# One block for the feed-forward network and the second attention, with their border woven together

## The chip, the cores and the metric

The kernel runs on one core of a Trainium2 chip. The metric is device time in microseconds (us), the median of several runs of the whole program; 1610.68 us before the change.

## The reference, cut to what matters

Two sequences of 512 tokens, width 512, all in float32, pass through four pre-normalised layers:

```python
x = x + _L0_attn_ref(_layernorm(x, axis=-1), L0_attn_wq, L0_attn_wk, L0_attn_wv, L0_attn_wo)
x = x + _L0_ffn_ref(_layernorm(x, axis=-1), L0_ffn_gate_t, L0_ffn_up_t, L0_ffn_down_t, L0_ffn_gate_s, L0_ffn_up_s, L0_ffn_down_s)
x = x + _L1_attn_ref(_layernorm(x, axis=-1), L1_attn_w_qkv, L1_attn_b_qkv, L1_attn_w_out, L1_attn_b_out)
x = x + _L1_ffn_ref(_layernorm(x, axis=-1), L1_ffn_A, L1_ffn_B, L1_ffn_Wr)
```

The change touches the border of the second line and the third. The network is `silu(x @ gate) * (x @ up)`, 1792 wide, times `down`. The second attention has 32 heads of 16, an ALiBi slope, a causal mask and biases on its projections.

## The kernel before, in words

Each layer is a phase in a `Block` of its own. A block ends with a barrier of all five engines; only then does the next phase's first instruction stand, on any engine or queue. Every float32 product is three matmuls: an operand is held as a rounded part `hi` and a rest `lo`, and `product` issues hi*hi, hi*lo and lo*hi (L64 to L66). Who makes `hi` and `lo` differs: ScalarE and VectorE for activations, GpSimd for the second attention's weights.

**The network** (`ffn0_phase`). 14 chunks of 128 of the 1792 hidden columns are made one after the other for both sequences. The first sequence's four output tiles are summed in four PSUM banks as the chunks come. The second sequence's hidden columns (`hidden1`) are kept, and its four output tiles are made after the last chunk, each in one run of 14 products = 42 matmuls, into the same four banks. So the first of them waits until VectorE has read the first bank (`out_scaled`). VectorE scales each finished tile by `down_s` (L953), adds it to `x` (L955) and takes its mean and variance (L76, L78).

**The norm** (`LayerNorm`). When all eight token tiles have their moments: a square root on ScalarE (L135), a reciprocal (L111), then for each tile a subtract-and-multiply on VectorE (L117), four transposes on TensorE (L150), `xT_hi` on ScalarE (L138) and `xT_lo` on VectorE (L124). TensorE waits for all eight tiles before its next matmul.

**The second attention** (`attention1_phase`). Heads are taken in 4 chunks of 8; a chunk has 16 units, 8 heads for each sequence, and `step(c, s)` runs a software pipeline: it scores unit s+3 (L1323), turns the probabilities of unit s+1 (L1336), attends unit s (L1348), and carries one piece of side work, such as the projection of the queries, keys or values of one sequence (`SIDE1`). Queries and keys are not used as they are made: SyncE writes them to DRAM (`write_out`), and GpSimd's queue reads them back into `stacked_q` and `stacked_k` in another layout, together with the slopes (`read_back`, L1234 to L1240). The first unit of each chunk and sequence waits for both. Steps 7 to 15 of chunk -1 are the preamble. GpSimd runs in program order: the first weights' halves, a memset of `stacked_q` (L1275), the read-backs of steps 7 and 8, that of step 15, eight additions of the output bias to `x` (L1283), the next query weights, and only then the read-back of step 0's keys.

## Time and profile before

| | before |
|---|---|
| median of 3 runs | 1610.68 us (1609.86 to 1612.18) |
| profiled execution's own time | 1609.08 us |
| its span, first to last instruction | 1607.2 us |
| TensorE (PE) busy | 1469.5 us, 91% |
| VectorE (DVE) busy | 1013.9 us, 63% |
| ScalarE (ACT) busy | 857.9 us, 53% |
| GpSimd (POOL) busy | 534.8 us, 33% |

"Busy" counts the instructions that compute. The shares are means over four phases: the first attention ends near 838 us, the network near 1089, the second attention near 1475. All times below are us from the start of the span of this one execution.

### The profile page before, as it was taken

Reading aid. Unit: us, or ns where it says so; the run is one execution under the profiler, and the core shown is the slowest. Engines: PE = TensorE matmul, PEld = TensorE weight load, DVE = VectorE, ACT = ScalarE, POOL = GpSimd, SP = SyncE. Lnnn points to the kernel's source line nnn. Section 1 sums busy time; section 2 is a strip of 40 time slices with the busy share of each in tenths; the row PEclk is TensorE's granted clock in tenths of the full one; section 3 lists DMA queues with packets and bytes.
Section 4 is the critical chain, followed back from the end, with each engine's and each line's share of the span. In section 5 each row is a group of like instructions: output and inputs, shape, how many; then the busy total and the mean of one; then the engine's idle time right before and its main releaser. Section 6 shows DMA issues by size and latency. Waiting matters only on the chain. (4 is left out here: it accounts for less than half of the span.)

```text
span 1607.2 us, 25387 instructions
## 1 busy us (share of the span) xinstructions
PE 1469.5 (91%) x7696; PEld 1208.1 (75%) x7696; DVE 1013.9 (63%) x2543; ACT 857.9 (53%) x2181; POOL 534.8 (33%) x465
## 2 busy tenths in 40 slices
PE   5999999999999999999778999995879999986798
PEld 3778888888888888888666888873667777764587
DVE  6676767676666676666544333344768888897543
ACT  2666555665566565556514233202768888894210
POOL 3673555545456554462400000005331313110500
PEclk9999999999999999999998999997889999997899
DMA  4010010101001010000002111005333444422000
GB/s 147 20 47 14 27 40 20 39 13 33 26 26 33 13 33 26 26 7 8 20 6 100 59 59 59 0 0 129 74 73 83 86 78 90 74 42 98 17 21 27
DMA packets 37468, 71.97 MB, mean 45 GB/s; under 512 B 4976, under 2 KB 5360, under 8 KB 36848
## 3 DMA queue, kind: packets, MB, share of 16 engines
q1 hardware_dynamic: 29664, 55.35, 11.3%
q0 software_dynamic: 7728, 15.73, 6.0%
q8 instruction: 33, 0.54, 0.1%
q14 instruction: 43, 0.35, 0.1%
HBM read 60.58 MB, written 10.49 MB: 44 GB/s over the span
## 5 line engine op out<-in xcount | busy, mean ns | idle before, releaser
L728 ACT ACTIVATE a_probs<-a_probs,a_least 128x512 f32<-128x512 f32 (+3 forms) x256 | 142.9, 559 | 175.6 <-DVE a_least L629 168.3
L377 POOL TENSOR_TENSOR a_rotated<-a_by_cos,a_by_sin 128x512 f32<-128x512 f32 x80 | 103.4, 1292 | 248.3 <-DVE a_by_sin L652 246.2
L637 DVE TENSOR_TENSOR a_probsT_lo<-a_ps_turn,a_probsT_hi 128x512 fp32r<-128x512 f32 (+3 forms) x256 | 118.7, 485 | 71.2 <-ACT a_probsT_hi L736 69.7
L736 ACT CAST a_probsT_hi<-a_ps_turn 128x512 fp32r<-128x512 f32 (+3 forms) x256 | 101.3, 426 | 102.0 <-PE a_ps_turn L526 102.0
L1532 ACT ACTIVATE a_probs<-a_probs,a_least 128x128 f32<-128x128 f32 (+3 forms) x256 | 142.3, 561 | 12.5 <-DVE a_least L1435 9.7
L1435 DVE CUSTOM_DVE_ANT_0 a_probs<-a_ps_score,a_causal 128x128 f32<-128x128 f32 (+3 forms) x256 | 117.2, 486 | 40.8 <-PE a_ps_score L1323 31.0
L782 ACT ACTIVATE a_probs<-a_probs,a_inverse 128x128 f32<-128x128 f32 (+3 forms) x256 | 123.2, 553 | 8.7 <-DVE a_inverse L690 7.5
L64 PE MATMUL a_ps_out<-a_wo_hi,a_attended_hi 128*128 128x512 f32 x256 | 105.5, 412 | 17.8 <-POOL a_wo_lo L371 15.6
L629 DVE CUSTOM_DVE_ANT_0 a_probs<-a_ps_score,a_causal 128x512 f32<-128x512 f32 (+2 forms) x192 | 101.1, 551 | 28.8 <-PE a_ps_score L66 28.7
L387 POOL TENSOR_TENSOR a_query_lo<-a_rotated,a_query_hi 128x512 fp32r<-128x512 f32 x64 | 82.6, 1290 | 105.8 <-ACT a_query_hi L748 105.8
L1443 DVE TENSOR_TENSOR a_probsT_lo<-a_ps_turn,a_probsT_hi 128x384 fp32r<-128x384 f32 (+1 forms) x192 | 108.9, 595 | 2.7 <-ACT a_probsT_hi L1541 2.6
L671 DVE TENSOR_TENSOR x<-a_ps_out,x 128x512 f32<-128x512 f32 x64 | 44.3, 692 | 104.9 <-PE a_ps_out L66 104.9
L64 PE MATMUL a_ps_proj<-xT_hi,a_wq_hi 128*128 128x512 f32 x256 | 110.3, 431 | 0.0
L1541 ACT CAST a_probsT_hi<-a_ps_turn 128x384 fp32r<-128x384 f32 (+1 forms) x192 | 85.7, 510 | 37.5 <-PE a_ps_turn L1336 37.4
L1336 PE MATMUL a_ps_turn<-ident,a_probs 128*128 128x128 f32 x640 | 93.2, 277 | 12.3 <-ACT a_probs L1532 12.2
L526 PE MATMUL a_ps_turn<-ident,a_probs 128*128 128x128 f32 x640 | 101.7, 273 | 1.1 <-ACT a_probs L782 1.1
L65 PE MATMUL a_ps_out<-a_wo_lo,a_attended_hi 128*128 128x512 f32 x256 | 102.7, 401 | 0.0
L66 PE MATMUL a_ps_out<-a_wo_hi,a_attended_lo 128*128 128x512 f32 x256 | 102.3, 400 | 0.0
L66 PE MATMUL a_ps_proj<-xT_hi,a_wq_lo 128*128 128x512 f32 x256 | 101.6, 397 | 0.0
L65 PE MATMUL a_ps_proj<-xT_lo,a_wq_hi 128*128 128x512 f32 x256 | 101.2, 395 | 0.0
L1323 PE MATMUL a_ps_score<-a_stacked_k,a_stacked_q 128*128 128x128 f32 (+3 forms) x256 | 77.6, 380 | 24.2 <-DMA a_stacked_k<-in_slope 13.2
L1216 POOL MEMSET a_zeros<- 128x512 f32 x1 | 0.5, 524 | 289.0 <-POOLq L811 289.0
(250 smaller groups left out, 4205.6 us busy)
## 6 DMA issues: line engine op xcount, KB each, us to landing
a_raw<-in_wq SPq DMA_DIRECT2D x36, 256.0 KB, 2.6
a_raw<-in_wo SPq DMA_DIRECT2D x36, 256.0 KB, 2.7
a_stacked_q<-a_spill_q POOLq DMA_DIRECT2D x48, 128.0 KB, 5.0
a_stacked_k<-a_spill_k POOLq DMA_DIRECT2D x24, 256.0 KB, 4.6
f_raw<-in_gate SPq DMA_DIRECT2D x14, 256.0 KB, 2.8
f_raw<-in_up SPq DMA_DIRECT2D x14, 256.0 KB, 3.0
f_raw<-in_down SPq DMA_DIRECT2D x14, 256.0 KB, 3.5
a_raw<-in_wk SPq DMA_DIRECT2D x12, 256.0 KB, 2.7
```

What stands on the lines that cost most here:

```text
L64: nc.tensor.matmul(out, left[0], right[0], start=start, stop=False)
L65: nc.tensor.matmul(out, left[0], right[1], start=False, stop=False)
L66: return nc.tensor.matmul(out, left[1], right[0], start=False, stop=stop)
L377: nc.gpsimd.tensor_tensor(rotated[:], by_cos[:], by_sin[:], ALU.add).then_inc(rotation_added, 1)
L526: last = nc.tensor.transpose(ps_turn[:, t % 2, (i - t) * P:(i - t + 1) * P], probs[:, u % 2, at:at + P], m.ident[:])
L637: nc.vector.tensor_tensor(probsT[1][:, t % 2, 0:w], ps_turn[:, t % 2, 0:w], probsT[0][:, t % 2, 0:w].bitcast(F32), ALU.subtract).then_inc( ...
L728: nc.scalar.activation(tile, tile, ACT.Exp, bias=least[:, slot, i:i + 1], scale=-1.0, accum_out=total[:, slot, i:i + 1]).then_inc(exp_done, 1)
L736: nc.scalar.copy(probsT[0][:, t % 2, 0:w], ps_turn[:, t % 2, 0:w]).then_inc(turned_hi, 1)
L782: nc.scalar.activation(tile, tile, ACT.Copy, scale=inverse[:, slot, i:i + 1]).then_inc(probs_ready, 1)
L1435: nc.vector.tensor_tensor_reduce(out=probs[:, u % 4, at:at + w], in0=ps_score[:, i % 2, 0:w], in1=causal[:, SEQ - w:SEQ], scale=-float(HD1 ...
L1443: nc.vector.tensor_tensor(probsT[1][:, u % 2, at], ps_turn[:, t, 0:TURNED_WIDTH[t]], probsT[0][:, u % 2, at].bitcast(F32), ALU.subtract).t ...
L1532: nc.scalar.activation(tile, tile, ACT.Exp, bias=least[:, u % 4, i:i + 1], scale=-1.0, accum_out=total[:, u // 4 % 2, i, u % 4:u % 4 + 1]) ...
```

## The change

The two phases become one function, `ffn0_attention1_phase`, with one block; the network becomes a class `Ffn0`. Both share one SBUF area and the same eight PSUM banks. `stacked_q`, `stacked_k`, `values`, `probs` and others lie in the place of the network's `down` and `hidden1` chunks, so a part is free once the last output tile has used a chunk (`chunk_free`); weights and small buffers lie in the place of `gate`, `up` and `raw`. The second sequence's tiles go to the banks of `ps_gate` and `ps_up` (`out_bank`). The norm of the second attention is cut in two halves of four tiles, one for each sequence, with a PSUM bank for each tile. The instructions keep their sizes and numbers, except that the load of `pick` and the memset of `stacked_q` are cut in two.

```diff
+    def second_sequence(self, pe, t, chunks):
+        nc, down, hidden1 = self.nc, self.down, self.hidden1
+        at = slice((t - QT) * P, (t - QT + 1) * P)
+        for f in chunks:
+            mm = product(nc, self.out_bank(t), (hidden1[0][:, f, at], hidden1[1][:, f, at]),
+                         (down[0][:, f, :], down[1][:, f, :]), f == 0, f == FC - 1)
+            if f == FC - 1:
+                mm.then_inc(self.out_done, 1)
+            elif t == NT - 1:
+                mm.then_inc(self.chunk_free, 1)
...
@@ tensor
-            norm.tensor(pe)
-            pe.wait_ge(pick_in, 16)
+            half = FC // 2
+            ffn.tensor(pe)
+            ffn.second_sequence(pe, 4, range(FC))
+            ffn.second_sequence(pe, 5, range(half))
+            norm.turn(pe, 0)
+            ffn.second_sequence(pe, 5, range(half, FC))
+            norm.ready(pe, 0)
+            side_work(-1, 7)
+            ffn.second_sequence(pe, 6, range(half))
+            side_work(-1, 8)
+            ffn.second_sequence(pe, 6, range(half, FC))
+            ffn.second_sequence(pe, 7, range(FC))
+            side_work(-1, 9)
...
+            pe.wait_ge(pick_in[0], 16)
+            pe.wait_ge(ffn.out_scaled, 6)
+            step(-1, 13)
+            side_work(-1, 10)
+            norm.turn(pe, 1)
+            pe.wait_ge(pick_in[1], 16)
             each_chunk(pe, step)
...
@@ vector
-            norm.vector(dve)
-            dve.wait_ge(consts_in, 16 * 3)
+            ffn.vector(dve)
+            for t in range(QT):
+                ffn.add_out(dve, t)
+            norm.shift(dve, 0)
+            norm.invert(dve, 0)
+            for t in range(QT):
+                norm.normalise(dve, t)
+            for t in range(QT):
+                norm.split(dve, t)
+            norm.normal_free(dve, 0)
+            ffn.add_out(dve, 4)
+            ffn.add_out(dve, 5)
+            dve.wait_ge(bias_in, 16)
...
+            step(-1, 8)
+            step(-1, 9)
+            ffn.add_out(dve, 6)
+            ffn.add_out(dve, 7)
+            norm.shift(dve, 1)
+            dve.wait_ge(causal_in, 16)
+            step(-1, 13)
+            norm.invert(dve, 1)
+            for t in range(QT, NT):
+                norm.normalise(dve, t)
+            step(-1, 11)
+            for t in range(QT, NT):
+                norm.split(dve, t)
+            norm.normal_free(dve, 1)
             each_chunk(dve, step)
...
@@ sync
+            ffn.sync(sp)
+            sp.dma_start(bias[:], dram["bias1"]).then_inc(bias_in, 16)
+
+            sp.wait_ge(ffn.weights_split, 3 * FC)
             for w, name in enumerate(("wq1", "wk1", "wv1")):
                 sp.dma_start(raw[:, w, :], dram[name][0]).then_inc(raw_in[w], 16)
...
@@ gpsimd
+            pool.wait_ge(ffn.made, 2 * FC)
             for what in ("wq", "wk", "wv"):
                 split(1, piece_count(0, what), what)
...
+            def prepare(b):
+
+                pool.wait_ge(ffn.chunk_free, 2 * b + 2)
+                pool.dma_start(stacked_q[96:P, b].rearrange("p a e n -> p (a e n)"),
+                               dram["pick"][:, b * 2 * PAIRS * SEQ:(b + 1) * 2 * PAIRS * SEQ]).then_inc(pick_in[b], 16)
+                nc.gpsimd.memset(stacked_q[0:96, b].rearrange("p a e n -> p (a e n)").bitcast(F32), 0.0).then_inc(stack_zero, 1)
+                pool.wait_ge(stack_zero, b + 1)
...
-            for s in (7, 8, 15):
-                read_back(-1, s)
+            prepare(0)
+            read_back(pool, -1, 7)
+            pool.wait_ge(ffn.chunk_free, 5)
+            read_back(pool, -1, 8)
+            prepare(1)
+            read_back(pool, -1, 15)
```

`second_sequence` appends tiles 4 to 7, the second sequence's, as matmuls; `side_work(-1, 7)`, `(-1, 8)`, `(-1, 9)` are the first projections of queries, keys and values; `step(-1, 13)` is the scoring of unit 0, and `side_work(-1, 10)` turns the values.

What moves on GpSimd, the engine that reads queries and keys back. Its first read-backs, before the change: the memset of both sequences' `stacked_q`, six DMAs of queries, then three of keys and one of slopes, which wait for the written keys.

```order
L1275 MEMSET a_stacked_q 96x8192
L1234 DMA a_stacked_q<-a_spill_q 16x4x512 [waits a1_stack_zero,a1_query_out]
L1234 DMA a_stacked_q<-a_spill_q 16x4x512 x5
L1238 DMA a_stacked_k<-a_spill_k 32x4x512 [waits a1_keys_out]
L1238 DMA a_stacked_k<-a_spill_k 32x4x512 x2
L1240 DMA a_stacked_k<-in_slope 32x2048
```

The same place after the change:

```order
L1333 DMA a_stacked_q<-in_pick 32x4096 [waits f0_chunk_free]
L1335 MEMSET a_stacked_q 96x4096
L1219 DMA a_stacked_q<-a_spill_q 16x4x512 [waits a1_stack_zero,a1_query_out]
L1219 DMA a_stacked_q<-a_spill_q 16x4x512 x5
L1223 DMA a_stacked_k<-a_spill_k 32x4x512 [waits f0_chunk_free,a1_keys_out]
L1223 DMA a_stacked_k<-a_spill_k 32x4x512 x2
L1225 DMA a_stacked_k<-in_slope 32x2048
```

The load of `pick`, which stood at the phase's start, has come behind the chunk count and ahead of a memset of half the size. Further down in GpSimd's program, at the second sequence's read-backs, before the change:

```order
L1234 DMA a_stacked_q<-a_spill_q 16x4x512 [waits a1_query_out]
L1234 DMA a_stacked_q<-a_spill_q 16x4x512 x5
L1283 TENSOR_TENSOR x<-x,a_out_bias 128x512 [waits ln_normal_done,a1_consts_in]
L1283 TENSOR_TENSOR x<-x,a_out_bias 128x512 x7
L1251 TENSOR_TENSOR a_wq_hi<-a_raw,a_zeros 128x512 [waits a1_wq_in,a1_side_made]
L1253 TENSOR_TENSOR a_wq_lo<-a_raw,a_wq_hi 128x512 [waits a1_piece_hi]
L1238 DMA a_stacked_k<-a_spill_k 32x4x512 [waits a1_keys_out]
L1238 DMA a_stacked_k<-a_spill_k 32x4x512 x2
L1240 DMA a_stacked_k<-in_slope 32x2048
```

After the change:

```order
L1219 DMA a_stacked_q<-a_spill_q 16x4x512 [waits a1_stack_zero,a1_query_out]
L1219 DMA a_stacked_q<-a_spill_q 16x4x512 x5
L1223 DMA a_stacked_k<-a_spill_k 32x4x512 [waits a1_keys_out]
L1223 DMA a_stacked_k<-a_spill_k 32x4x512 x2
L1225 DMA a_stacked_k<-in_slope 32x2048
L1305 TENSOR_TENSOR x<-x,a_out_bias 128x512 [waits ln_normal_done,a1_out_bias_in]
L1305 TENSOR_TENSOR x<-x,a_out_bias 128x512 x7
L1296 TENSOR_TENSOR a_wq_hi<-a_raw,a_zeros 128x512 [waits a1_wq_in,a1_side_made]
L1298 TENSOR_TENSOR a_wq_lo<-a_raw,a_wq_hi 128x512 [waits a1_piece_hi]
```

The key read-back now stands ahead of the eight bias additions and the two weight halves. On ScalarE, from the square root's table to the first exponentials of the second attention, after the change (`f_ps_out` and `f_ps_up` are the shared banks):

```order
L155 ACT_TABLE_LOAD
L155 ACTIVATE ln_deviation<-ln_shifted 128x4 [waits ln_var_done]
L162 CAST xT_hi<-f_ps_out 128x4x128 [waits ln_turned_done] x4
L1666 CAST a_query_hi<-a_biased_q 128x512 [waits a1_side_read]
L1666 CAST a_keys_hi<-a_biased_k 128x512 [waits a1_side_read]
L155 ACTIVATE ln_deviation<-ln_shifted 128x4 [waits ln_var_done]
L1679 COPY a_values_turned<-f_ps_out 128x512 [waits a1_side_made]
L1683 CAST a_values<-f_ps_out 128x32x16 [waits a1_side_made]
L162 CAST xT_hi<-f_ps_up 128x4x128 [waits ln_turned_done] x2
L162 CAST xT_hi<-f_ps_out 128x4x128 [waits ln_turned_done] x2
L1641 ACT_TABLE_LOAD
L1641 ACTIVATE a_probs,a_total<-a_probs,a_least 128x128 [waits a1_score_masked]
```

Before, the eight casts of `xT_hi` all stood ahead of the queries, and the exponentials' table load stood right behind the cast of `a_values`; now four casts stand between them.

## Rows read from the trace of the kernel before

**Rows 1.** Busy time of each engine by stretch; PEclk is the granted clock
```profile
core 0: us, PE busy (x) PEld busy (x) DVE busy (x) ACT busy (x) POOL busy (x), PEclk, DMA share, GB/s
...
1048.00:1087.00 39.00, 38.62 (x168) 31.47 (x168) 15.01 (x28) 0.00 (x0) 0.00 (x0) 1.00 0.00 0
1087.00:1103.00 16.00, 8.64 (x34) 5.89 (x33) 13.80 (x22) 6.18 (x10) 8.00 (x8) 0.63 0.63 165
...
1177.00:1475.00 298.00, 268.28 (x1680) 209.12 (x1678) 254.47 (x746) 248.93 (x710) 53.77 (x78) 0.98 0.35 67
```

**Rows 2.** Timeline of TensorE over the border: start, duration, instruction, idle before
```profile
1048.38 0.47 PE L64 MATMUL f_ps_out<-f_down_hi,f_hidden_hi 128*128 128x512 f32 x1 [0.99 <-DVE f_hidden L953]
1048.69 0.40 PE L65 MATMUL f_ps_out<-f_down_lo,f_hidden_hi 128*128 128x512 f32 x1
...
1086.69 0.40 PE L66 MATMUL f_ps_out<-f_down_hi,f_hidden_lo 128*128 128x512 f32 x1
1092.14 1.97 PE L150 MATMUL a_ps_turn<-ident,a_probs 128*128 128x128 f32 x8 [5.06 <-DVE a_probs L117]
...
1103.56 0.63 PE L65 MATMUL a_ps_side<-xT_lo,a_wq_hi 128*128 128x512 f32 x1
1103.98 0.63 PE L66 MATMUL a_ps_side<-xT_hi,a_wq_lo 128*128 128x512 f32 x1
...
1127.97 0.77 PE L1323 MATMUL a_ps_score<-a_stacked_k,a_stacked_q 128*128 128x128 f32 x2 [10.25 <-DMA a_stacked_k<-in_slope]
...
1133.02 1.70 PE L1336 MATMUL a_ps_turn<-ident,a_probs 128*128 128x128 f32 x7
```

**Rows 3.** Timeline of TensorE around the second sequence's first unit
```profile
1159.08 0.98 PE L1336 MATMUL a_ps_turn<-ident,a_probs 128*128 128x128 f32 x7 [1.46 <-ACT a_probs L1532]
...
1163.23 0.98 PE L1336 MATMUL a_ps_turn<-ident,a_probs 128*128 128x128 f32 x7 [0.52 <-ACT a_probs L1532]
1172.35 0.77 PE L1323 MATMUL a_ps_score<-a_stacked_k,a_stacked_q 128*128 128x128 f32 x2 [8.14 <-issue]
...
1176.53 0.93 PE L1336 MATMUL a_ps_turn<-ident,a_probs 128*128 128x128 f32 x7
```

**Rows 4.** Timeline of GpSimd: its memset, its read-backs, the bias additions
```profile
1103.99 6.93 POOL L1275 MEMSET a_stacked_q<- 96x8192 f32 x1
1114.14 3.07 POOL L1234 DMA_DIRECT2D a_stacked_q<-a_spill_q  x6 [3.22 <-DMA a_spill_q<-a_query_lo]
1120.83 1.62 POOL L1238 DMA_DIRECT2D a_stacked_k<-a_spill_k  x3 [3.61 <-DMA a_spill_k<-a_keys_lo]
1122.43 0.52 POOL L1240 DMA_DIRECT2D a_stacked_k<-in_slope  x1
1152.58 9.98 POOL L1283 TENSOR_TENSOR x<-x,a_out_bias 128x512 f32<-128x512 f32 x8
...
1166.69 0.51 POOL L1240 DMA_DIRECT2D a_stacked_k<-in_slope  x1
```

**Rows 5.** VectorE beside GpSimd: an operation with both inputs in SBUF
```profile
301.94 1.29 POOL L377 TENSOR_TENSOR a_rotated<-a_by_cos,a_by_sin 128x512 f32<-128x512 f32 x1
...
302.15 1.23 DVE L629 CUSTOM_DVE_ANT_0 a_probs<-a_first_tile,a_causal 128x128 f32<-128x128 f32 x1 [0.19 <-DVE a_first_tile L625]
```

**Rows 6.** Landing of all DMAs into `a_stacked_k`
```profile
DMA to landing us min/median/max: 3.3/5.1/7.6
```

**Rows 7.** Single operations of VectorE and ScalarE that the sum uses
```profile
1099.86 0.53 DVE L117 TENSOR_SCALAR a_probs<-x,moments,ln_inverse 128x512 f32<-128x512 f32 x1
...
1131.03 0.08 DVE L1435 DVE_READ_ACCUMULATOR2_ANT a_least<- 128x1 f32 x1
...
1101.60 0.58 ACT L138 CAST xT_hi<-a_ps_score 128x512 fp32r<-128x512 f32 x1 [0.47 <-PE a_ps_score L150]
...
1118.37 1.28 ACT L1532 ACT_TABLE_LOAD   x1
```

**Rows 8.** The page's group of all exponentials of the second attention
```profile
L1532 ACT ACTIVATE a_probs<-a_probs,a_least 128x128 f32<-128x128 f32 (+3 forms) x256 | 142.3, 561 | 12.5 <-DVE a_least L1435 9.7
```

623 lines of the change are left out of this document (338 added, 285 removed).

## The prediction, on record before the changed kernel ran

> **What bounds the kernel now.** I began with the page, where TensorE is busy for 91% of the span, so that a border between two phases matters only where TensorE stands still or runs at the lower clock. The chain that ended last lies in the last phase alone and says nothing of this border. So I took the busy time by stretch, then TensorE's timeline, then those of the engines that release it.
>
> Until 1087 TensorE issues the second sequence's 168 matmuls without a gap, at a granted clock of 1.00 (2.4 GHz) [rows 1]. They start 0.23 us apart: 166 steps in 38.0 us [rows 2]. Nothing else is behind them: GpSimd does nothing in that stretch and ScalarE nothing [rows 1]. Then come, one after the other, the last tile's moments, the barrier, the norm, three projections, and the trip of queries and keys through DRAM. TensorE idles 5.06 us, does the norm at a clock of 0.63 on average [rows 1, 2], projects at a pitch of 0.42 us (1103.56 to 1103.98, 1.2 GHz), and idles 10.25 us more until the slopes, the last of the keys' DMAs, have landed [rows 2]. From the last of the 168 matmuls (1086.69) to the first score (1127.97) are 41.3 us, in which TensorE has only 36 matmuls and 36 transposes to do.
>
> A second gap follows. At 1164.2 TensorE wants the second sequence's first score and gets it at 1172.35, 8.14 us later [rows 3]. The row names no releaser, but GpSimd's rows do: the keys' read-back stands behind 9.98 us of bias additions and two weight halves, its slopes are issued at 1166.69 and the score comes 5.66 us after that [rows 3, 4]. After 1177 TensorE, VectorE and ScalarE are busy for 90, 85 and 84% [rows 1], and no gap of this size is left.
>
> **The change part by part.** The instructions are the same, so the sum is of waits. I walk along the new path in the times of this trace.
>
> *Start of tile 4.* It no longer waits 0.99 us for `out_scaled` [rows 2], only for `hidden_lo`, which VectorE ends directly before the scaling of the first bank, so some 0.7 us of the gap could go. But the first weights' halves now run on GpSimd at that moment, and `hidden_lo` has both inputs in SBUF. Such an operation of VectorE took 1.23 us beside a running GpSimd operation, for 128x128, and ended with it [rows 5]. So I give back most of the 0.7: start at 1048.2, bounds 1047.7 and 1048.9. The Trainium skill has this as a rule (SBUF — State Buffer, "Who interferes with whom"): a VectorE instruction with two SBUF inputs contends with a GpSimd instruction that reads SBUF, and one in a two-port mode with any GpSimd instruction. It speaks against this change, which puts GpSimd's splits and memsets beside VectorE's additions to `x` and its norm; rows 5 agree with it, and by it each addition beside a split may wait for the end of that split.
>
> The additions have room for that. VectorE does the first four tiles in about 9 us (28 instructions, seven tiles' worth, are busy for 15.0 us [rows 1]) and the norm's half in 3 more, so normalised tiles are there by 1060, or by 1062 if GpSimd costs it 2 us; TensorE asks for them after 63 matmuls, at 1048.2 + 14.4 = 1062.6. The norm of the first half therefore costs TensorE only its 16 transposes at 0.14 us (7 take 0.98) [rows 3], 2.2 us, and casts and `xT_lo` lie under the 21 matmuls (4.8 us) behind them. The queries' and keys' additions, halves and writes lie under tile 6, with some 10 us to spare before they are read back.
>
> *Start of tile 7.* 126 matmuls of tiles 4 to 6 and 24 of queries and keys, 150 x 0.229 = 34.35 us, and 2.2: 1084.75. Two chunks of tile 7 more (6 matmuls, 1.4 us) release GpSimd at 1086.15.
>
> *The read-back, the path from here on.* The load of `pick` 0.5 us as any issue (0.52); half of the memset's 6.93 us, 3.47; six query issues 3.07; three key issues 1.62 [rows 4]: the slopes are issued at 1094.8. From that issue to the first score were 5.54 us before (1122.43 to 1127.97) [rows 2, 4] and 5.66 at the other gap: first score at 1100.4. Before, it was at 1127.97: 27.6 us are won here. Meanwhile TensorE ends tile 7 and the values at 1084.75 + 54 x 0.229 = 1097.1 and waits some 3.3 us; that is what is left of 41 us. Bounds: the landings into `a_stacked_k` were 3.3 to 7.6 us [rows 6]; here 1.75 MB of queries and keys are issued back to back, so the upper end is open: -2.2 to +2.1 us.
>
> The Trainium skill prices it otherwise (DMA: Bandwidth & Descriptors, "Anatomy of one DMA — SWDGE (gpsimd) path"): 2.0 us, plus the bytes at 436 bytes per ns, for a DMA of GpSimd. For the slopes' 0.26 MB that is 2.6 us, an estimate by that page, and TensorE's own work would then end last, at 1097.1: the whole gain would be 3.3 us larger. The rows, 5.5 us twice, decide for the sum.
>
> *From the first score to the first turn.* Before, 5.05 us (1127.97 to 1133.02) [rows 2]. Now the second half of the norm stands between, and with it what was parallel becomes serial: the four masks of unit 0 take 3.1 us (1131.03 against 1127.97) [rows 2, 7]; reciprocal and first normalised tile 0.8 (0.53 for the tile); then four tiles, by TensorE at the low clock 4.3 us (8 transposes 1.97, the rows' pitch of 1.06 a tile), by VectorE's 0.53 a tile 2.1; the last cast 0.58; then ScalarE's table load of 1.28, which lay hidden in a wait before; then four exponentials of 0.56 [rows 2, 7, 8]. With the mean of the two paces, 3.2: 3.1 + 0.8 + 3.2 + 0.6 + 1.3 + 2.25 = 11.25, and 0.2 for hand-overs. The first turn is at 1111.9, against 1133.02: **21.1 us** remain of the 27.6. Bounds: pace of the transposes ±1.1, the landing -2.2 and +2.1, VectorE and GpSimd ±0.5: 18 to 24.
>
> *The second gap.* The stretch from 1133.02 to 1163.23 has the same rows in both kernels. Where the score waits now, GpSimd issues the keys' read-back directly behind the queries' (which ends at 1152.58): the keys' three DMAs and the slopes are issued by 1155 (3.07 and 1.62 us of issues as before, if the written keys have landed by then, as an estimate), landed at 1160.7 by the 5.66, before the 1164 at which they are wanted. Then the next turn follows after the pace of the step before, 1163.23 - 1159.08 = 4.15, at 1167.4 instead of 1176.53 [rows 3]: 9.1 us, in which the return from the low clock is contained. The keys' 1 MB now share the queues with the next weights and the queries, so I take off 0.6: **8.5 us**, bounds 5 (three more us of landing eat the margin and some) and 9.4. The bias additions and weight halves, now behind, end some 13 us later, near 1168; the next chunk's queries want them at 1175 in the same shifted times. That margin hides them; if it were gone, it would cost what it falls short.
>
> Sum: 21.1 + 8.5 = 29.6 us. Against the profiled execution's own time, 1609.08, that is 1579.5. The median of the runs stands 1.6 above it, so **1581.1 us**.
>
> **The rivals.** A measurement of this kernel tells some 0.2%, 3.2 us, from no change.
>
> (a) *Both gaps close as summed*: 1577 to 1586. Chance 0.63.
>
> (b) *The second gap stays in part, 8.5 becomes 2 to 5.* The keys wait behind the queries' and weights' transfers, or GpSimd, in program order, is late with something that is queued behind it. For it: the 1164 of demand is only 3.5 us after my landing, and the longest landing was 7.6 [rows 6]. Then 2 to 5 us of the 8.5 are won, 1584.6 to 1587.6, and with a late first landing up to 1590. Chance 0.17.
>
> (c) *Landings are as quick as the page has them, or the clock stays up*: TensorE idles under 1 us before the first score and does the transposes at 2.4 GHz: 3.3 + 1.1 more, 1573 to 1577. Against it: two gaps that took 5.5 us. Chance 0.10.
>
> (d) *The gain is mostly given back by VectorE.* It now carries the adds of tiles 6 and 7, the norm's halves and the masks in one fixed order, and each waits for the one before; a step in the wrong order (shift of half 1 stuck behind GpSimd's memset of 3.47 us, then ScalarE's root, then its copy of the values) lies just under the landing of 1100.4. Were it 5 to 15 us late: 1586 to 1596. Chance 0.07.
>
> (e) *Slower.* The stretch now issues projections, transposes and tiles of three kinds. If TensorE's clock fell to 1.2 GHz in it, each of the 204 matmuls would take 0.42 instead of 0.229 us, up to +39 us, 1620; from 155 matmuls at the low clock on (29.6 / 0.19) the kernel is slower. Against it: the clock stayed at 1.00 over the 0.99 us gap at 1047 [rows 1, 2], and the new order has no longer one before 1097. Chance 0.03.
>
> **How the numbers follow.** The likeliest case gives 1581.1, its own range 1577 to 1586. With (c)'s nearer half and most of (b) the range is 1575 to 1589; outside are (d), (e) and the far ends. Faster by over 0.2% covers (a), (b), (c) and nearly all of (d): 0.96; within 0.2%: 0.01; slower 0.03.
>
> **What would show it.** In the trace of the changed kernel: 168 + 36 matmuls with no gap over 1 us from 1048 to 1097; a gap of 2 to 5 us before the first score, released by the slopes' DMA; the first turn of probabilities near 1112, behind a table load of ScalarE; no gap of 8 us at the ninth unit's score, near 1142; and from there the same rows some 30 us earlier. I am wrong if the first score comes before 1097 or after 1103, if VectorE releases TensorE inside the woven stretch for more than 1 us, or if a gap reappears at a later chunk's first score, where GpSimd's program is the same as before.

## The result: 1591.2 us, 19.6 us faster, where 29.6 were forecast

The changed kernel took 1591.22 us in the median of its first four runs (1589.31 to 1595.56), beside 1610.85 before: a ratio of 0.988, interval 0.986 to 0.990. The sign and the place of the gain were as forecast; the gain was a third smaller than forecast, and 1591.2 lies outside the range of 1575 to 1589. In a second set of runs the same kernel took 1588.2 us beside 1610.0 (0.987, 0.985 to 0.988), 21.8 us faster and just inside that range. The profiled execution is the slowest of the first four: 1595.56 us by its own time, a span of 1593.4 us. It already runs 2.7 us late when the border begins (its last halves of the network's hidden values are 2.7 us behind those of before), so 2.7 us are taken off where its times are held against those of before.

TensorE's timeline over the border and the two gaps (start, duration, instruction, idle before it and what ended that) answers to [rows 2, 3]:

```profile
1050.75 0.50 PE L64 MATMUL f_ps_gate<-f_chunks 128*128 128x512 f32 x1 [0.68 <-DVE f_chunks L973]
...
1106.51 0.76 PE L1387 MATMUL f_ps_gate<-a_stacked_k,a_stacked_q 128*128 128x128 f32 x2 [7.46 <-DMA a_stacked_k<-in_slope]
...
1118.41 1.73 PE L1400 MATMUL f_ps_out<-ident,a_probs 128*128 128x128 f32 x7 [1.92 <-ACT a_probs L1641]
...
1144.52 0.98 PE L1400 MATMUL f_ps_out<-ident,a_probs 128*128 128x128 f32 x7 [1.45 <-ACT a_probs L1641]
...
1148.66 0.98 PE L1400 MATMUL f_ps_out<-ident,a_probs 128*128 128x128 f32 x7 [0.55 <-ACT a_probs L1641]
1150.66 0.47 PE L1387 MATMUL f_ps_gate<-a_stacked_k,a_stacked_q 128*128 128x128 f32 x2 [1.01 <-issue]
...
1155.89 1.14 PE L1387 MATMUL f_ps_gate<-a_stacked_k,a_stacked_q 128*128 128x384 f32 x2 [3.85 <-DVE a_least L1529]
...
1157.90 1.44 PE L1400 MATMUL f_ps_out<-ident,a_probs 128*128 128x128 f32 x7
```

Between 1050.75 and 1106 no row of TensorE shows an idle time: the woven stretch holds. The first score still waits for the slopes, as forecast, but 7.46 us and not 3.3. The ninth unit's score (1150.66) no longer waits 8 us but 1.01; its third and fourth parts wait 3.85 us more, and not for a DMA but for VectorE's mask.

GpSimd's timeline, against [rows 4]:

```profile
1088.49 0.65 POOL L1333 DMA_DIRECT2D a_stacked_q<-in_pick  x1 [32.00 <-PE f_ps_up L66]
1089.13 3.54 POOL L1335 MEMSET a_stacked_q<- 96x4096 f32 x1
1093.33 3.02 POOL L1219 DMA_DIRECT2D a_stacked_q<-a_spill_q  x6 [0.66 <-POOL a_stacked_q L1335]
...
1097.95 0.52 POOL L1225 DMA_DIRECT2D a_stacked_k<-in_slope  x1
1098.45 0.52 POOL L1333 DMA_DIRECT2D a_stacked_q<-in_pick  x1
...
1135.06 3.01 POOL L1219 DMA_DIRECT2D a_stacked_q<-a_spill_q  x6 [32.57 <-DMA a_spill_q<-a_query_lo]
1142.10 1.61 POOL L1223 DMA_DIRECT2D a_stacked_k<-a_spill_k  x3 [4.03 <-DMA a_spill_k<-a_keys_lo]
1143.70 0.51 POOL L1225 DMA_DIRECT2D a_stacked_k<-in_slope  x1
1144.23 9.90 POOL L1305 TENSOR_TENSOR x<-x,a_out_bias 128x512 f32<-128x512 f32 x8
1154.09 1.25 POOL L1296 TENSOR_TENSOR a_wq_hi<-a_raw,a_zeros 128x512 fp32r<-128x512 f32 x1
```

The bias additions, a stretch without a pause from 1144.23 to 1154.09, now stand exactly over the time in which VectorE divides the first half of the attention. VectorE's timeline there:

```profile
1149.43 0.63 DVE L1546 TENSOR_REDUCE a_summed<-f_ps_up 128x256 f32<-128x512 f32 x1
1150.16 5.47 DVE L1551 TENSOR_TENSOR a_result<-a_summed,a_inverse 128x256 f32<-128x256 f32 x1
1155.55 0.28 DVE L1529 CUSTOM_DVE_ANT_0 a_probs<-f_ps_gate,a_causal 128x128 f32<-128x128 f32 x1
```

The multiply at L1551 has both inputs in SBUF. Its group over the whole trace, of the kernel before and then of the changed one (minimum, median and maximum in ns, first and last start):

```profile
L1457 DVE TENSOR_TENSOR a_result<-a_summed,a_inverse x16: 424/425/1492, 1164.7 to 1461.3; 128x256 f32<-128x256 f32 x16
```

and changed:

```profile
L1551 DVE TENSOR_TENSOR a_result<-a_summed,a_inverse x16: 424/426/5466, 1150.2 to 1448.6; 128x256 f32<-128x256 f32 x16
```

Thirteen of the sixteen take 0.43 us at most, two take 0.99 and 1.44 beside GpSimd's weight halves, and the one beside the bias additions takes 5.47. It ends at 1155.63, 0.29 us behind the first weight half (`wq_hi`, 1154.09 to 1155.34), and behind that half GpSimd pauses for the first time since 1144.23, for 0.08 us. In VectorE's order the masks of the ninth unit stand behind it, and TensorE, which needs a free score bank, behind those.

Where the 13.8 us of difference between the two spans come from: to the first turn of probabilities 14.61 (1133.02 to 1118.41), at the second gap 4.06 (from the turn before it to the turn behind it 13.30 before [rows 3], 9.24 now), in the expert phase, whose code is the same, 1.59, and of that 6.42 are lost again between 1157.90 and the end of the second attention (305.1 us against 298.7), and 0.04 between the gaps.

### The profile page after: what moved, and what is told of

Its sections match the earlier page's. It is cut to its first block and busy times, and to the rows that moved or that the text cites. A ratio compares the mean times of both kernels' runs of the same rounds, so it can differ in the third digit from the quotient of the medians.

```text
span 1593.4 us, 25389 instructions
## 1 busy us (share of the span) xinstructions
PE 1469.0 (92%) x7696; PEld 1212.6 (76%) x7696; DVE 1021.9 (64%) x2545; ACT 857.5 (54%) x2182; POOL 536.5 (34%) x467
## 3 DMA queue, kind: packets, MB, share of 16 engines
HBM read 60.58 MB, written 10.49 MB: 45 GB/s over the span
## 5 line engine op out<-in xcount | busy, mean ns | idle before, releaser
L1529 DVE CUSTOM_DVE_ANT_0 a_probs<-f_ps_gate,a_causal 128x128 f32<-128x128 f32 (+3 forms) x256 | 117.1, 486 | 32.8 <-PE f_ps_gate L1387 22.9
L1537 DVE TENSOR_TENSOR a_probsT_lo<-f_ps_out,a_probsT_hi 128x384 fp32r<-128x384 f32 (+1 forms) x192 | 108.9, 596 | 2.3 <-ACT a_probsT_hi L1650 2.2
L1400 PE MATMUL f_ps_out<-ident,a_probs 128*128 128x128 f32 x640 | 94.4, 280 | 13.8 <-ACT a_probs L1641 13.7
L1650 ACT CAST a_probsT_hi<-f_ps_out 128x384 fp32r<-128x384 f32 (+1 forms) x192 | 85.7, 510 | 32.7 <-PE f_ps_out L1400 32.7
L555 PE MATMUL a_ps_turn<-ident,a_probs 128*128 128x128 f32 x640 | 101.5, 273 | 1.1 <-ACT a_probs L811 1.1
L1387 PE MATMUL f_ps_gate<-a_stacked_k,a_stacked_q 128*128 128x128 f32 (+3 forms) x256 | 77.8, 382 | 20.7 <-DMA a_stacked_k<-in_slope 12.3
L1400 PEld LDWEIGHTS f_ps_out<-ident,a_probs 128*128 128x128 f32 x640 | 75.2, 143 | 25.2 <-ACT a_probs L1641 11.3
```

The costliest lines, as they stand in the source:

```text
L555: last = nc.tensor.transpose(ps_turn[:, t % 2, (i - t) * P:(i - t + 1) * P], probs[:, u % 2, at:at + P], m.ident[:])
L1400: last = nc.tensor.transpose(ps_turn[:, t, to:to + P], probs[:, u % 4, at:at + P], m.ident[:])
L1529: nc.vector.tensor_tensor_reduce(out=probs[:, u % 4, at:at + w], in0=ps_score[:, i % 2, 0:w], in1=causal[:, SEQ - w:SEQ], scale=-float(HD1 ...
L1537: nc.vector.tensor_tensor(probsT[1][:, u % 2, at], ps_turn[:, t, 0:TURNED_WIDTH[t]], probsT[0][:, u % 2, at].bitcast(F32), ALU.subtract).t ...
```

## The experiments

Fifteen variants and the changed kernel once more. Times are medians. "The landing" is the time from the issue of the slopes' DMA to the first score of TensorE, unless said otherwise; "the step over the gap" is the time from the turn of probabilities before the second gap to the turn behind it; "the release" is the issue of the first load of `pick` or, where GpSimd's memset comes first, the start of that memset.

### The changed kernel again

> The changed kernel, nothing altered. Its profiled execution was its slowest run (1595.56 us against 1589.31 to 1592.02 in the others), and lost 4.0 us at the scores of the third chunk and 2.0 at those of the fifth, where TensorE waited 2.76 and 2.12 us for the slopes and then ran at 1.2 GHz for a while; before the change the same waits were 1.43 and 1.49 and the clock stayed up. Theory that this is chance in the landings (they differ from run to run): median 1590 to 1592 and, in this profile, at least one of the two waits under 1.6 us with no slow clock behind it. Rival, that the change itself makes these landings late: both waits above 2 us again. The first score (1106.5, 8.5 us after the slopes' issue) and the multiply of a_result of 5.47 us at 1150 come back in either case.

1588.22 us (1585.18 to 1589.06), ratio 0.9869 (0.9854 to 0.9883). The first score comes 8.0 us behind the slopes' issue, the multiply takes 5.88 us and the step over the second gap 9.65. The waits that the expectations place in "the third chunk" and "the fifth", or in "the chunks 2 and 4", are those of the second sequence's first score in the second and in the third of the four chunks (at 1237.84 and 1322.90 in the profile of the result). Here they are 2.57 and 1.52 us, with the granted clock at 1.00 behind both. The second is under 1.6, as the theory of chance asks, but the median lies 1.8 us below its range, and both waits are again above those of the profile before (1.43 and 1.49). So this run does not settle it. What stands before the border differs from trace to trace too: the last casts of the network's hidden values begin between 1043.0 and 1049.0 us in the sixteen traces of changed kernels, whose code is the same up to there, and at the fortieth instruction of ScalarE (63.1 to 67.3 us) 4.2 us of that are already there.

### The second part of the change alone

In the kernel before, only the order of GpSimd in the first chunk:

```diff
                 more = not isinstance(c, int) or c < CHUNKS1 - 1
+                first = isinstance(c, int) and c == 0
+                if first:
+                    read_back(c, 0)
+                    pool.wait_ge(consts_in, 16 * 3)
+                    pool.wait_ge(m.ln_semaphores[LN_SEMAPHORES.index("normal_done")], 3 * NT)
+                    for t in range(NT):
+                        nc.gpsimd.tensor_tensor(m.x[:, t, :], m.x[:, t, :], out_bias[:], ALU.add).then_inc(bias_added, 1)
                 if more:
                     wait(pool, side_made, side_count(c - 1, 15))
                     split(c + 2, piece_count(c + 1, "wq"), "wq")
-                read_back(c, 0)
+                if not first:
+                    read_back(c, 0)
...
-            pool.wait_ge(consts_in, 16 * 3)
-            pool.wait_ge(m.ln_semaphores[LN_SEMAPHORES.index("normal_done")], 3 * NT)
-            for t in range(NT):
-                nc.gpsimd.tensor_tensor(m.x[:, t, :], m.x[:, t, :], out_bias[:], ALU.add).then_inc(bias_added, 1)
             chunk(0)
```

> The kernel before with one thing of the change: in the first chunk GpSimd reads the keys back ahead of the bias additions and of the split of the first weights. Theory A, VectorE's multiply into a_result with two inputs in SBUF is held by the bias additions of GpSimd that now run beside it, so the second gap shrinks by 4 us and not by 8.5: 1606 to 1608, with that multiply at 4 to 6 us. Theory B, my prediction: the gap closes, 8.5 us won, 1601.5 to 1603, with the multiply at 0.4 to 1.5 us.

1607.01 us over 12 runs (1602.0 to 1610.2), ratio 0.9979 (0.9968 to 0.999): 3.0 us won. That fits theory A. The step over the gap is 8.69 us (13.30 before), and VectorE's multiply is the slow one:

```profile
1166.29 4.92 DVE L1461 TENSOR_TENSOR a_result<-a_summed,a_inverse 128x256 f32<-128x256 f32 x1
```

### The first part alone

```diff
                 if first:
-                    read_back(pool, c, 0)
                     add_out_bias()
                 if more:
                     wait(pool, side_made, side_count(c - 1, 15))
                     split(c + 2, piece_count(c + 1, "wq"), "wq")
-                if not first:
-                    read_back(pool, c, 0)
+                read_back(pool, c, 0)
```

> The changed kernel with GpSimd's old order in the first chunk: bias additions and the split of the first weights ahead of the keys' read-back; all else as changed. That is the first part of the change alone. By the trace of the changed kernel the second part is worth 4.0 us: 1594 to 1596. By my prediction it is worth 8.5: 1599 to 1600.

1592.32 us (1588.7 to 1595.3), ratio 0.9899 (0.9885 to 0.9913). That is 17.7 us under the kernel before, and 4.1 above the changed kernel in the same set of runs. The wait of the ninth score is back, 7.87 us, the multiply takes 0.97 us at most, and the step over the gap is 13.05. So the two parts are worth 17.7 and 4.1 us, not 21.1 and 8.5. It came out 1.7 us below what was expected for 4.0.

### The bias additions where GpSimd is idle

```diff
             prepare(1)
+            add_out_bias()
             read_back(pool, -1, 15)
...
                 if first:
                     read_back(pool, c, 0)
-                    add_out_bias()
```

> The changed kernel with the bias additions directly behind the preparation of the second half of the queries' buffer, in the 30 us in which GpSimd waits for the next queries; no other line altered. Theory A (the additions hold VectorE's multiply, and the masks and TensorE's score behind it): the multiply falls from 5.47 to about 0.4 to 1.5 us, the wait of 3.85 us at TensorE and the slow clock behind it go, 4 to 5 us won, 1585.5 to 1587.5. Theory B (the multiply is slow for another reason, or something else then holds the score): no change, 1590 to 1592. It is slower if the additions now hold VectorE's norm or casts instead: over 1592.

1585.04 us (1584.6 to 1587.4), 3.2 under the changed kernel. The additions run from 1108.5 to 1118.4. Nothing else was touched, and the multiply is short:

```profile
1148.37 0.93 DVE L1551 TENSOR_TENSOR a_result<-a_summed,a_inverse 128x256 f32<-128x256 f32 x1
```

The turns of TensorE on both sides of the gap are at 1146.87 and 1151.99: a step of 5.12 us, where 9.24 and 9.65 were, and 4.8 forecast. The granted clock stays at 1.00 behind the score; in the changed kernel it was 0.50 from 1156 to 1158. This shows the cause of the missing 4 us: the multiply beside the additions. The keys' landing still holds the score 1.45 us here, within that step. The additions start when the second half's normalised tiles are done, and VectorE's `xT_lo`, which now run beside them, lose nothing by it: 0.69 us each, as in the changed kernel.

### The second load of `pick` out of the way

```diff
+            pool.wait_ge(score_made, 12)
             prepare(1)
...
-            pe.wait_ge(pick_in[1], 16)
...
+                    if isinstance(cu, int) and (cu, u) == (0, HPC):
+                        pe.wait_ge(pick_in[1], 16)
```

> The changed kernel with GpSimd's preparation of the second half of the queries' buffer (its load of pick, 0.5 MB, and its memset) held until three units are scored; TensorE waits for that load only at the ninth unit. In the changed kernel this load is issued 0.5 us behind the slopes and shares the queues with them. Theory P, it delays the slopes: they land 5.5 to 6.5 us after their issue instead of 8.5, and the first score comes 2 to 3 us earlier against the end of tile 7, for 1585.5 to 1587. Theory Q, it is the 1.75 MB of queries, keys and slopes issued back to back: still 8 to 9 us, and the time is that of the changed kernel, 1588 to 1591. In either case VectorE's shift of the second half, 3.75 us before, takes under 0.5 us, and gives nothing, since it is done long before its inverse is wanted.

1590.67 us (1589.2 to 1592.3): nothing won. The landing is 7.71 us, against 8.56, 8.00, 8.23 and 8.28 in the four traces until then, but 7.76 and 7.89 in two that ran in one set with it and leave the load in place. Theory P's 5.5 to 6.5 us are refuted; the landing is a little below the 8 to 9 of theory Q. What this load costs the slopes is within what the landings differ by from trace to trace. VectorE's shift of the second half takes 0.17 us here, as expected.

### The exponential's table early

```diff
             step(-1, 11)
+            nc.scalar.activation(total[:, 1, 3, 3:4], norm.shifted[:, norm.columns(1)][:, 0:1], ACT.Exp)
             norm.round(act, 1)
```

> The changed kernel with one more instruction of ScalarE: an exponential of one element a partition, behind the copy of the first values, whose result nobody reads. It pulls the load of the exponential's table into the time in which ScalarE waits for the second half's transposes. If that load (1.28 us) and what follows it set the first turn, as the prediction's serial sum has it, the first turn comes 1.0 to 1.3 us sooner behind the first score (11.9 us before): 10.6 to 10.9, and the median falls by about as much, 1587 to 1590. If VectorE or TensorE sets that turn: no change.

The median, 1589.54 us (1585.6 to 1590.5), cannot tell. The trace can: from the first score to the first turn 10.49 us (1104.18 to 1114.67), 11.90 and 11.91 in the two traces of the changed kernel. ScalarE's rows, of the changed kernel and of this one:

```profile
1114.08 0.58 ACT L162 CAST xT_hi<-f_ps_out 128x512 fp32r<-128x512 f32 x1 [0.27 <-PE f_ps_out L178]
1114.68 1.28 ACT L1641 ACT_TABLE_LOAD   x1
1115.98 0.40 ACT L1641 ACTIVATE a_probs<-a_probs,a_least 128x128 f32<-128x128 f32 x1
```

```profile
1107.92 1.28 ACT L1702 ACT_TABLE_LOAD   x1
...
1111.76 0.59 ACT L162 CAST xT_hi<-f_ps_out 128x512 fp32r<-128x512 f32 x1 [0.27 <-PE f_ps_out L178]
1112.24 0.41 ACT L1641 ACTIVATE a_probs<-a_probs,a_least 128x128 f32<-128x128 f32 x1
```

The serial term of the prediction is right, table load included: with the load taken out of the way, the turn comes 1.4 us sooner.

### The keys first in every chunk

```diff
+                if not first:
+                    read_back(pool, c, 0)
                 if more:
                     wait(pool, side_made, side_count(c - 1, 15))
                     split(c + 2, piece_count(c + 1, "wq"), "wq")
-                if not first:
-                    read_back(pool, c, 0)
```

> The changed kernel with GpSimd's read-back of the keys ahead of the split of the next weights in every chunk, as the change does in the first chunk alone. In the chunks 2 and 4 (of the eight) the split waits 5.6 us for its weights and the keys behind it, so that TensorE stands 2.1 to 2.8 us at the first score in one trace and 1.5 to 2.6 in another, sometimes with the slow clock behind it. Theory: these two waits go, 3 to 6 us won over the changed kernel, 1583 to 1587, and the runs lie closer together. Rival: the keys' reads then share the queues with the weights' loads, both land later, and the time stays, 1588 to 1591.

1585.66 us (1584.2 to 1586.2), ratio 0.9846 (0.9831 to 0.9861): 2.6 under the 1588.22 of the changed kernel in the set of runs before. The two intervals overlap a little, so the median alone leaves it open; the traces don't. The two waits are 0.86 and 1.44 us. In the changed kernel GpSimd waits for weights in front of the keys that TensorE needs next:

```profile
1219.39 3.04 POOL L1219 DMA_DIRECT2D a_stacked_q<-a_spill_q  x6 [31.34 <-DMA a_spill_q<-a_query_lo]
1228.08 1.27 POOL L1296 TENSOR_TENSOR a_wq_hi<-a_raw,a_zeros 128x512 fp32r<-128x512 f32 x1 [5.65 <-DMA a_raw<-in_wq]
1229.42 1.29 POOL L1298 TENSOR_TENSOR a_wq_lo<-a_raw,a_wq_hi 128x512 fp32r<-128x512 f32 x1
1230.65 1.64 POOL L1223 DMA_DIRECT2D a_stacked_k<-a_spill_k  x3
```

```profile
1237.84 0.79 PE L1387 MATMUL f_ps_gate<-a_stacked_k,a_stacked_q 128*128 128x128 f32 x2 [2.76 <-DMA a_stacked_k<-in_slope]
```

In that trace the clock falls behind this wait. The busy time by stretch (length, then busy time and instructions of PE, PEld, DVE, ACT, POOL, the granted clock, DMA):

```profile
1226.00:1234.00 8.00, 7.12 (x50) 5.57 (x48) 7.57 (x23) 7.95 (x25) 5.84 (x7) 1.00 0.81 177
1234.00:1238.00 4.00, 1.24 (x10) 0.98 (x8) 3.44 (x8) 2.08 (x7) 3.84 (x4) 0.93 0.75 130
1238.00:1244.00 6.00, 6.00 (x21) 4.42 (x22) 3.77 (x12) 3.35 (x10) 0.07 (x1) 0.50 0.01 3
1244.00:1248.00 4.00, 4.00 (x29) 3.30 (x28) 3.32 (x12) 3.46 (x9) 0.12 (x1) 0.97 0.00 0
```

TensorE idles 2.76 us and then works six at 1.2 GHz. Before the change the same wait was 1.43 us and the clock stayed at 1.00 behind it. The length of the wait alone does not decide this: in the changed kernel's second trace the clock stayed at 1.00 behind 2.57 us, and with the load of out_bias late it fell behind 2.35. The stretch from the first turn behind the second gap to the end of the second attention (298.7 us in the profile before) separates the two orders without an overlap: 300.0 to 305.1 us, 302.6 in the mean, in the twelve traces of changed kernels that keep the weights ahead of the keys; 298.6, 299.0, 298.1 and 297.6 in the four that have the keys first. The kernel before, which has the weights ahead too, shows 298.7 in its profile and 303.1 with the first chunk's order alone. So the two orders lie 4.3 us apart in the mean. How much of the profile's late 6.4 us belongs to this is not shown, for the kernel before has the same order there.

### All four

> The changed kernel with the four edits together: bias additions early (measured alone: 3.2 us), the second pick held, the keys first in every chunk, the table early. If each gives what its theory says and they add: 3.2 + 2.5 + 4 + 1.2, about 11 us below the changed kernel, 1576 to 1579. If only the bias additions matter: 1585. If keys-first alone fails but the others hold: 1581 to 1583.

1582.62 us (1578.1 to 1584.9), ratio 0.9819. The four do not add. The time is in the range written down for the case that keys-first fails, but the waits that it was to shorten are short here too (0.54 and 0.71 us). The ninth unit's score waits again, for a DMA this time, 3.37 us:

```profile
1150.51 0.77 PE L1389 MATMUL f_ps_gate<-a_stacked_k,a_stacked_q 128*128 128x128 f32 x2 [3.37 <-DMA a_stacked_k<-in_slope]
```

The held load pushes the bias additions to 1123.5 to 1134.4, so that the queries' read-back waits for them and the keys' follows it at once; its slopes are issued at 1139.04, their own landing takes 11.2 us, and the score comes 11.5 us behind the issue.

### Three edits, and a shared memset

Three edits are the four without the held load. The memset is cut so:

```diff
             ffn.add_out(dve, 6)
+            dve.wait_ge(ffn.chunk_free, 2)
+            nc.vector.memset(stacked_q[0:96, 0, PAIRS // 2:PAIRS].rearrange("p a e n -> p (a e n)").bitcast(F32), 0.0).then_inc(stack_zero, 1)
             ffn.add_out(dve, 7)
```

> The changed kernel with three edits: bias additions early, the keys first in every chunk, the table early; the second pick is not held. With all four the bias additions stood behind that pick, took until 1134.4 and made the queries' and keys' read-back of the first chunk late (slopes issued 1139.0, score 11.5 us later, 3.4 us of waiting). If that was the cost of holding the pick, the wait at the ninth unit is under 2 us again and the median is 1578 to 1581. If keys-first has the same effect without it: as with all four, 1581 to 1584.

1579.60 us (1578.2 to 1584.0), ratio 0.982 (0.980 to 0.984). The ninth score waits 1.21 us, which fits the held `pick` as what made it late (one trace of each). The medians do not tell the two kernels apart: their ratios to the kernel before are both 0.982. This is some 9 us below the changed kernel's second set. TensorE still waits 5.74 us for the first score.

> The changed kernel with the first memset (3.54 us of GpSimd, between the release of the memory and the first read-back) cut in two: GpSimd clears two head pairs, VectorE, idle there for 7 us, the other two, between its additions of tiles 6 and 7. Theory: GpSimd's part takes 1.8 us, all that GpSimd issues comes 1.7 us sooner, and so do the slopes and the first score against the release of the memory (18.0 us from the issue of pick to the first score in the changed kernel, then 16.3): 1586.5 to 1589.5. Rival: the two memsets keep each other off the memory and run one after the other, so that nothing is won and VectorE's additions come later: 1588 to 1591.

The changed kernel with the shared memset alone: 1588.12 us (1584.4 to 1589.7), nothing won. GpSimd's memset takes 1.83 us beside VectorE's 1.76, they overlap, and the slopes are issued 8.13 us behind the load of `pick` instead of 9.46; but the landing is now 9.40 us instead of 6.8 to 8.6. Neither theory: the issues came sooner, the first score did not (17.53 us behind the release, 17.2 to 18.0 in six traces without the shared memset and 16.3 with three edits).

> Three edits (bias additions early, keys first, table early) and the shared memset. If the shared memset gives its 1.7 us here too: 1.0 to 2.5 us below the kernel with three edits. If TensorE, which ends tile 7 and the values some 7 us before the first score, is still waiting by then, nothing stands in the way of it. No gain, if the two memsets hold each other.

1579.22 us (1577.9 to 1584.4), ratio 0.981 (0.979 to 0.983): the same as with three edits. The landing is again 9.40 us, and the first score comes 17.54 us behind the release.

### What makes the slopes late

> The changed kernel with the first read-back of the queries (six DMAs, 0.75 MB) cut to the first 128 of 512 columns, same number of DMAs and of rows in each; the rest of that half keeps its zeros, so the first chunk's probabilities of that sequence are other numbers and nothing else is. From the slopes' issue to the first score the six traces with that part unaltered show 7.8 to 8.6 us, and two with the second pick out of the way 7.3 and 7.7; before the change it was 5.5 with the queries long landed. Theory Q, the bytes of the burst are what the slopes queue behind: 0.56 MB less, at the 200 to 290 GB/s that the trace shows there, brings the score 2 to 2.8 us nearer, 5.3 to 6.2 us. Rival, the number of DMAs or of their descriptors counts, not the bytes: 7.5 to 8.6 us as before.

The edit is `n = slice(0, P)` for the six DMAs of the first read-back. One run, 1587.5 us. The landing is 5.84 us (1094.46 to 1100.30), in the range expected for the bytes; the number of packets from 1080 to 1112 us is 1489, as in the changed kernel. The page's list of DMA issues over the border, of the changed kernel and of this one (KB each, median us from issue to landing):

```profile
a_stacked_q<-a_spill_q POOLq DMA_DIRECT2D x6, 128.0 KB, 4.8
a_stacked_k<-a_spill_k POOLq DMA_DIRECT2D x3, 256.0 KB, 7.1
a_out_bias<-in_out_bias SPq DMA_DIRECT2D x1, 256.0 KB, 3.9
a_stacked_k<-in_slope POOLq DMA_DIRECT2D x1, 256.0 KB, 8.4
```

```profile
a_stacked_k<-a_spill_k POOLq DMA_DIRECT2D x3, 256.0 KB, 4.2
...
a_stacked_k<-in_slope POOLq DMA_DIRECT2D x1, 256.0 KB, 5.7
a_stacked_q<-a_spill_q POOLq DMA_DIRECT2D x6, 32.0 KB, 2.0
```

With the queries light, keys and slopes land as they did before the change (5.1 us median of all [rows 6]).

> The changed kernel with the first load of pick cut to 128 of 512 columns (0.125 MB in place of 0.5) and issued behind the first memset, which clears its rows too; the masks of the first chunk's first sequence are other numbers by that. Theory T, the transfers ahead in GpSimd's queue, that of pick among them, set when the slopes land: from the slopes' issue to the first score 6.2 to 7.2 us, against 7.8 to 8.6 with the load uncut. Rival, that load is long through when the queries' come: 7.8 to 8.6 as before. The issue itself moves by no more than 0.5 us.

One run, 1597.65 us beside 1614.87 of the kernel before. Theory T is refuted: 10.1 us from the slopes' issue (1096.67 to 1106.78), later than with the load uncut.

> The same with the first memset shared between GpSimd and VectorE. With the load of pick uncut the shared memset brought the slopes' issue 1.3 us forward and the first score not at all (9.4 us behind that issue, twice). By theory T those 1.3 us were eaten by the transfer of pick, and come back here: slopes' issue to first score 6.2 to 7.5 us, and release of the memory to first score under 16 us against 17.2 to 18.0. Rival, the landing hangs on something outside GpSimd's queue that does not move with its issues: 8.5 us or more from the slopes' issue.

One run, 1593.32 us. Refuted too: 9.71 us, and 18.5 from the release to the first score. Both are what the rival expects, that something which does not move with GpSimd's issues sets the landing; what that would be is not shown. Why the small load made it worse I can't say; its pieces are 512 bytes in place of whole rows, and it now stands directly in front of the queries.

> The changed kernel with SyncE's load of out_bias (0.25 MB, issued 1 us before the queries' read-back begins, on SyncE's queue) moved behind the write of the next queries, some 40 us later. Theory U, two queues at work beside each other slow the read-back: from the slopes' issue to the first score 6.8 to 7.4 us, against 7.8 to 8.6 in six traces with that load in place. Rival, GpSimd's queue alone sets the landing: 7.8 to 8.6.

One run, 1589.79 us beside 1611.17 of the kernel before. The rival: 7.99 us (1093.18 to 1101.17), as with the load in place.

> The changed kernel with the load of out_bias late, the second pick held until three units are scored, and the first memset shared with VectorE, so that only the first load of pick, issued 3.5 us earlier, and the queries, keys and slopes themselves are in the queues. If the read-back is slow for what runs beside it: 6 to 7 us from the slopes' issue, under 15.5 us from the release of the memory to the first score (17.2 to 18.0 before). If the six queries' DMAs, three keys' and the slopes, 1.75 MB back to back, are slow by themselves: 8 us or more from the slopes' issue, and 16 us or more from the release.

One run, 1585.81 us; 7.75 us from the slopes' issue, 15.9 from the release (1083.06 to 1098.94). Both lie between the two expectations. The landing behind the slopes' issue stays near 8 us with the second `pick` and `out_bias` out of the way, which speaks for the burst of queries, keys and slopes itself. The first score comes 1.3 us sooner behind the release than with the held load alone (17.2), one trace of each; traces that leave all this alone differ by 1.7 us (16.3 to 18.0), so that gain is not shown.

From the first of the queries' issues to the first score it is 11.5 to 13.2 us in eleven traces with all the queries' bytes, 10.4 with the light queries, but 14.0 twice with the shared memset and 14.7 and 14.3 with the small `pick`, whose queries' bytes are the same or whose queue holds fewer. So the queries' bytes are one part of the landing, and another 1 to 2 us of it stay unexplained.

## Why the prediction was right in direction and too large

**The woven stretch: right.** Tile 4 starts at 1048.05 in the times of before (1050.75 less 2.70), forecast 1048.2. The contention by which I gave back most of the 0.7 us is there: the last `hidden_lo` takes 1.04 us and the first two additions to `x` 1.06 and 1.40, all 0.69 elsewhere, beside GpSimd's splits. This agrees with the Trainium skill ("SBUF — State Buffer", "Who interferes with whom"), by which a VectorE instruction with two SBUF inputs contends with a GpSimd instruction that reads SBUF. The norm's first half, tile 7 and GpSimd's release (1085.8 for 1086.15) are as walked.

**The issue of the slopes: right.** 1095.25 for 1094.8; the difference is mostly an idle 0.66 us between memset and queries, which I had not counted.

**The landing behind it: mis-sized.** The step "From that issue to the first score were 5.54 us before" took 8.56 in the profile and 6.8 to 8.6 in the seven traces that leave that part alone. In the times of before the first score stands at 1103.8 (1106.51 less 2.70), forecast 1100.4: behind the 1103 that I had named as a sign of being wrong. The 5.54 and 5.66 were read where the queries had long landed; here 0.75 MB of them lie in front. I had named the 1.75 MB as an open upper end of 2.1 us, and it came out 3.0. One trace shows that the queries' bytes make most of it: without three quarters of them the landing is 5.84 us. Shrinking or moving the loads of `pick` and `out_bias` did not shorten it beyond the spread. Why it was 9.4 to 10.1 us in four traces stays open. The Trainium skill's price ("DMA: Bandwidth & Descriptors", "Anatomy of one DMA — SWDGE (gpsimd) path"), 2.6 us for the slopes alone, is less than half of what the lists above show: 8.4 us, and 5.7 with light queries. Even by that price (an estimate: 1094.8 and 2.6) the slopes would have landed at 1097.4, so that TensorE's own work, ending at 1097.1, would not have ended last, as I had written.

**From the first score to the first turn: right.** 11.45 us forecast, 11.9 measured. Together the first part is worth 17.3 us in the profile (14.61 and the 2.70), and 17.7 by the experiment, not 21.1: the landing is 3.0 of the 3.8 that are missing.

**The second gap: the step failed.** "Then the next turn follows after the pace of the step before" took for granted that nothing but the keys' landing held the ninth unit. The keys did land nearly in time (an idle 1.01 us at 1150.66, 6.96 us behind the slopes' issue at 1143.70). That was close: I had them issued directly behind the queries, by 1155, and GpSimd waited 4.03 us for the written keys, so that the slopes were issued at 1158.3 in the times of before (1143.70 and the 14.61), and the 3.5 us of margin were used up. The rest of the gap, 4.1 of the 5.1 us by which the step of 9.24 exceeds the pace of 4.15, has another mechanism than rival (b) named, though (b)'s size came: the multiply beside the bias additions. I had written the rule down, for the norm and the additions to `x`, and had said of the bias additions only that they "end some 13 us later", with an eye on who waits for them, not on who runs beside them. What was to be looked up: which VectorE instructions with two SBUF inputs lie within the ten microseconds into which a ten-microsecond block of GpSimd is moved. That this multiply is the cause is shown from both sides: alone in the old kernel (the multiply takes 4.92 us, 3.0 us are won), and removed in the new (0.93 us, the step at 5.12).

**The rest.** 17.3 and 4.1 make 21.4 us; the second set of runs has 21.8, the first 19.6. The profile's own 13.5 (1609.08 to 1595.56) is lower still by its late start and by the spread of the later chunks, where GpSimd waits for the weights in front of the keys and the clock falls behind some of TensorE's waits. I had said that a gap at a later chunk's first score would prove me wrong, "where GpSimd's program is the same as before": the gaps are there in the kernel before as well, at 1.4 and 1.5 us in its profile and 2.3 and 2.4 in that of the kernel with the first chunk's order alone. Whether the change makes them longer in the mean stays open: two traces, 298.7 and 303.1 us over that stretch, do not tell. Rivals (c), (d) and (e) did not come. Of (d) the block is real, VectorE's shift of the second half takes 3.75 us under GpSimd's memset, but its inverse is wanted only 7 us after it ends.

## What to carry to other kernels

A block of GpSimd work that is moved off one wait lands on something: list the VectorE instructions with both inputs in SBUF that now run beside it, for one instruction of 0.4 us can take as long as the rest of the block and what follows it without a pause, and all that VectorE does next waits with it. A landing time read from a trace holds for the queue as it stood there; behind a burst on the same queue, count the bytes in front as well, and leave room: here they explain most of the delay in one trace, and not the 9.4 to 10.1 us of four others. And where two stretches of the same code differ by 5 us between traces, a profile of one execution is no ruler for the last 5 us of a sum.

## What was new of the hardware

Four instructions show GpSimd's hold on VectorE, each beside its usual time: 0.42 to 5.47 us (two SBUF inputs, beside eight additions in a row), 0.17 to 3.75 us (a 128x4 shift under a memset of 3.54 us), 0.69 to 1.04 and to 1.40 us (beside weight splits of 1.29, which themselves took up to 1.73). Beside the weight splits the same multiply took 0.5 to 1.5 us; that it is the row without a pause that holds it so long is the likeliest reading. In all twelve traces in which the multiply meets the additions it ends 0.29 us behind the end of `wq_hi`, where GpSimd's first pause of 0.08 us stands, and takes 4.9 to 5.9 us. Against it stands one multiply of 1.37 us (small `pick`, 1237.10), which ended between two halves without a pause. No kernel with a pause put between the additions was run. A memset of GpSimd and one of VectorE on different pairs of the same tile ran side by side: GpSimd's took 1.83 us for half of what takes it 3.54 alone, VectorE's 1.76. And 1.3 us of earlier issues on a busy queue brought the first score forward by nothing in two traces; in one with 0.5 MB less queued behind it, it came 1.3 us sooner, which is within the spread.
